# Attention scores as one fp32 product, and the feed-forward weight splits moved between stages

## The reference, cut to what matters

```python
h = tok(x)                                  # layer norm of shifted patches, times W
h = concat([cls_tok, h])                    # 16 x 37 x 192
n = layernorm(h)
q = n @ w_q.T + b_q; k = n @ w_k.T + b_k; v = n @ w_v.T + b_v
scores = einsum('bqhd,bkhd->bhqk', q, k) / sqrt(16) + mask
h = h + (softmax(scores) @ v) @ w_o.T + b_o
n = layernorm(h)
h = h + alpha * shared(n) + (1 - alpha) * routed(n)
```

## Time and profile before

| what | before |
|---|---|
| median of three runs | 172.95 us |
| the profiled execution's own time | 172.75 us |
| its span, first to last instruction | 170.9 us |
| mean granted TensorE clock | 0.970 of full |
| busy: PE, weight loads, DVE, ACT, POOL | 149.0, 115.8, 121.2, 90.8, 41.2 us |
| transfers | 16.89 MB, mean 99 GB/s |

### The profile page before, as it was taken

One profiled execution on the slowest core, in us unless ns is written; L12 is line 12 of the kernel. 1 busy time (PEld: TensorE's weight loads), 2 busy tenths in 40 slices (PEclk: granted clock), 3 DMA queues, 4 the chain that ended last, 5 costly groups with the idle time before them and its releaser, 6 DMA issues.

```text
span 170.9 us, 4275 instructions
## 1 busy us (share of the span) xinstructions
PE 149.0 (87%) x1714; PEld 115.8 (68%) x1714; DVE 121.2 (71%) x297; ACT 90.8 (53%) x198; POOL 41.2 (24%) x55
## 2 busy tenths in 40 slices
PE   0439999998899889669998689999899999999992
PEld 0218777943569778568954468788777778888781
DVE  6299969898999997933377399876795752533753
ACT  0598779544669255251328768666645444343340
POOL 0000010000000000000000044337947858578430
PEclk9999999999999999965699999999999999999999
DMA  5999946700000000029960000048100000000003
GB/s 165 390 362 364 333 86 196 312 3 0 0 0 4 4 4 4 4 45 391 333 249 0 4 0 0 8 172 335 62 4 0 0 0 4 4 0 4 0 0 106
DMA packets 7391, 16.89 MB, mean 99 GB/s; under 512 B 800, under 2 KB 3612, under 8 KB 7372
## 3 DMA queue, kind: packets, MB, share of 16 engines
q1 hardware_dynamic: 7012, 16.29, 27.3%
q10 hardware_dynamic: 360, 0.34, 0.7%
HBM read 16.15 MB, written 0.47 MB: 97 GB/s over the span
## 4 chain that ended last, share of the span: by engine, by line
PE 57%; DVE 24%; ACT 7%; issue 5%; ACTq 3%; POOL 2%; DVEq 0%; POOLq 0%
PE PS L582 20%; PE PS L610 11%; PE PS L324 3%; PE PS L415 3%; DVE xsq L1130 3%; DVE mx L1126 2%; DVE piece L968 2%; PE PS L477 2%; PE PS L345 2%; PE PS L347 2%; PE PS L348 2%; PE PS L427 2%; DVE hn L1053 2%; PE PS L311 2%; POOL vhl L865 1%
## 5 line engine op out<-in xcount | busy, mean ns | idle before, releaser
L874 POOL TENSOR_TENSOR kq<-vhl,kq 128x296 f16<-128x296 f32 x35 | 28.7, 819 | 93.8 <-ACT kq L826 93.8
L1271 DVE SCALAR_TENSOR_TENSOR vhl<-PS,vhl 128x296 f32<-128x296 f32 x36 | 16.7, 465 | 21.0 <-POOL vhl L865 12.1
L819 ACT ACTIVATE vhl<-PS 128x296 f32<-128x296 f32 x36 | 14.9, 416 | 26.2 <-PE PS L582 26.2
L826 ACT ACTIVATE kq<-vhl 128x296 f16<-128x296 f32 x36 | 16.0, 446 | 5.7 <-DVE vhl L1271 5.7
L865 POOL TENSOR_TENSOR vhl<-vhl,xs 128x296 f32<-128x296 f32 x14 | 12.6, 901 | 5.5 <-issue 4.8
L1260 DVE TENSOR_TENSOR vhl<-vhl,xs 64x296 f32<-64x296 f32 (+1 forms) x18 | 10.2, 566 | 2.8 <-ACT vhl L819 2.6
L582 PE MATMUL PS<-XAh,piece 128*128 128x296 f16 x48 | 10.0, 289 | 2.0 <-DVE vhl L1271 1.9
L582 PE MATMUL PS<-XAh,slab 128*128 128x296 f16 x48 | 10.0, 290 | 0.9 <-DVE vhl L1271 0.9
L345 PE MATMUL PS<-whl,xhl 128*128 128x193 f16 (+1 forms) x40 | 10.5, 262 | 0.0
L925 DVE SCALAR_TENSOR_TENSOR we<-slab,gbs,we 128x192 f32<-128x192 f32 x24 | 8.1, 409 | 3.3 <-ACT we L666 3.3
L347 PE MATMUL PS<-whl,xhl 128*128 128x193 f16 (+1 forms) x40 | 10.4, 261 | 0.0
(11 more groups left out here) (217 smaller groups left out, 409.0 us busy)
## 6 DMA issues: line engine op xcount, KB each, us to landing
slab<-in_w_inner_dram SPq DMA_DIRECT2D x3, 960.0 KB, 9.7
xs<-gate_rows_dram SPq DMA_DIRECT2D x8, 296.0 KB, 5.5
xs<-in_x_inner_dram SPq DMA_DIRECT2D x3, 592.0 KB, 10.7
stage<-in_f_a_dram SPq DMA_DIRECT2D x2, 768.0 KB, 4.7
stage<-in_f_b_dram SPq DMA_DIRECT2D x2, 768.0 KB, 6.3
stage<-in_f_d_dram SPq DMA_DIRECT2D x2, 576.0 KB, 8.0
xhl<-in_f_a_dram SPq DMA_DIRECT2D x1, 768.0 KB, 5.2
xhl<-in_f_b_dram SPq DMA_DIRECT2D x1, 768.0 KB, 6.9
```

The lines of the kernel that those rows point to most:

```text
L819: A(silu[:, i % 2, :], PS[:, 3 + 2 * (i % 2), 0:HALF], ACT.Silu, scale=1.0 / XW).then_inc(S["a_silu"], 1)
L826: A(ah[:, f % ABUF, half * HALF:(half + 1) * HALF], hf[:, i % 3, :], ACT.Copy).then_inc(S["a_ah"], 1)
L874: G.tensor_tensor(al[:, f % ABUF, cols], hf[:, i % 3, :], ah[:, f % ABUF, cols], ALU.subtract).then_inc(S["g_al"], 1)
L1271: V.scalar_tensor_tensor(out=hf[:, i % 3, :], in0=PS[:, 4 + 2 * (i % 2), 0:HALF], scalar=SH / XW, in1=src[:, i % 2, :], op0=ALU.mult, op1= ...
```

## The change

Keys and queries are written once, in fp32, by ACT (`K32`, `Q32`); `kq_low` is gone from DVE, and product `f` waits for ACT alone. A score is one fp32 product instead of two f16 products, with scale factors that suit. ACT runs steps 2 to 5 of `ffn_high` between and right behind the key and query copies, where it ran them behind all of these. DVE runs steps 0 to 2 of `ffn_low` in the part of the keys, queries and values and steps 3, 4 and 5 behind `differences(2)`, `differences(3)` and `normalise(2)`; before, steps 0 and 1 stood ahead of `differences(0)`, steps 2 to 4 ahead of `differences(3)` and step 5 behind `differences(3)` and `normalise(1)`. The `own_values` steps 4 to 7 stand behind `differences(0)` and `differences(1)`, two each. On PE `wo(0)` is issued before `av(6)`. The loop of the rounds on ACT is written in another way, but its instructions keep their order.

```diff
@@ -53,10 +53,11 @@
 PIECES = 3
 PT_ = FT // PIECES
 
-SX, SW, SPIX, SPW, SK, SQ, SP_, SV, SCTX, SH = 64.0, 64.0, 16.0, 256.0, 16.0, 4.0, 256.0, 16.0, 16.0, 16.0
+SX, SW, SPIX, SPW, SK, SH, QKS = 64.0, 64.0, 16.0, 256.0, 16.0, 16.0, 32.0
 XW = SX * SW
 
 GATE_STEP = 6
+ABUF = 3
 CONSTS = 128 + 2 * CHUNKS + 1 + D + GROUPS + EXPERTS
 FRONT = 3 * P
 
...
@@ -147,10 +148,9 @@
         WC = sb("WC", [CROWS, AW], F16)
 
         KFC = 2 * LANES * 4 * BLOCK
-        kh = xsq[:, KFC:KFC + GROUPS * N // 2].bitcast(F16).rearrange("p (g n) -> p g n", g=GROUPS)
-        kq = sb("kq", [P, 3 * GROUPS * N // 2 + 192])
-        kqv = kq[:, 0:3 * GROUPS * N // 2].bitcast(F16).rearrange("p (k g n) -> p k g n", k=3, g=GROUPS)
-        KK, Q1, Q2 = kqv[:, 0], kqv[:, 1], kqv[:, 2]
+        kq = sb("kq", [P, ABUF * NPAD])
+        K32 = xsq[:, KFC:KFC + GROUPS * N].rearrange("p (g n) -> p g n", g=GROUPS)
+        Q32 = kq[:, 0:GROUPS * N].rearrange("p (g n) -> p g n", g=GROUPS)
         vhl = sb("vhl", [P, IMAGES * LANES * VW])
         vv = vhl[0:BLOCK, :].rearrange("p (b r c) -> p b r c", b=IMAGES, r=LANES)
         SCOLS = 2 * BLOCK
...
@@ -407,7 +406,7 @@
                 c0 = (QC if q else KC) + g * P
                 if f >= 4:
                     q4, g4, half4 = kq_product(f - 4)
-                    pe.wait_ge(S["v_q2" if q4 else "v_kk"], GROUPS * half4 + g4 + 1)
+                    pe.wait_ge(S["a_q" if q4 else "a_k"], GROUPS * half4 + g4 + 1)
                 cols = slice(half * HALF, (half + 1) * HALF)
                 for i, (w, x) in enumerate(zip(wparts(c0, c0 + P), xparts(cols))):
                     if f in (0, 6):
...
@@ -440,13 +439,12 @@
                         b = 2 * (2 * u + pair) + bi
                         tok = slice(b * POSITIONS, (b + 1) * POSITIONS)
                         for g in range(GROUPS):
-                            for Q in (Q1, Q2):
-                                for r in range(LANES):
-                                    rows = slice(32 * r, 32 * r + 32)
-                                    col = pair * BLOCK + g * POSITIONS
-                                    last = mm(PS[64 * bi:64 * bi + POSITIONS, 3 + r, col:col + POSITIONS],
-                                              Q[rows, g, tok], KK[rows, g, tok], start=False, stop=(Q is Q2),
-                                              skip_group_check=True)
+                            for r in range(LANES):
+                                rows = slice(32 * r, 32 * r + 32)
+                                col = pair * BLOCK + g * POSITIONS
+                                last = mm(PS[64 * bi:64 * bi + POSITIONS, 3 + r, col:col + POSITIONS],
+                                          Q32[rows, g, tok], K32[rows, g, tok], start=False, stop=True,
+                                          skip_group_check=True)
                 last.then_inc(S["p_s"], 1)
 
             def pt(p):
...
@@ -506,8 +504,8 @@
                 values(i)
             pe.wait_ge(S["v_mk"], 1)
             pe.wait_ge(S["v_jr"], 2)
-            pe.wait_ge(S["v_kk"], 6)
-            pe.wait_ge(S["v_q2"], 6)
+            pe.wait_ge(S["a_k"], 6)
+            pe.wait_ge(S["a_q"], 6)
             scores(0)
             for i in range(4, 7):
                 values(i)
...
@@ -529,11 +527,11 @@
                 if u >= 2:
                     ct(2 * u - 4)
                     ct(2 * u - 3)
+            wo(0)
             av(6)
             av(7)
             ct(4)
             ct(5)
-            wo(0)
             wo(1)
             ct(6)
             ct(7)
...
@@ -750,9 +748,9 @@
                 cols = slice(half * HALF, (half + 1) * HALF)
                 act.wait_ge(S["p_q" if q else "p_k"], GROUPS * half + g + 1)
                 if q:
-                    A(Q1[:, g, cols], PS[:, 3 + f % 4, 0:HALF], ACT.Copy, scale=SQ / XW).then_inc(S["a_q1"], 1)
+                    A(Q32[:, g, cols], PS[:, 3 + f % 4, 0:HALF], ACT.Copy, scale=QKS / XW).then_inc(S["a_q"], 1)
                 else:
-                    A(kh[:, g, cols], PS[:, 3 + f % 4, 0:HALF], ACT.Copy, scale=kscale).then_inc(S["a_kh"], 1)
+                    A(K32[:, g, cols], PS[:, 3 + f % 4, 0:HALF], ACT.Copy, scale=1.0 / XW).then_inc(S["a_k"], 1)
 
             root(0)
             ffn_high(0, 0)
...
@@ -768,19 +766,21 @@
             high_parts(0, (1, 2, 0), 1)
             for f in range(3, 12):
                 kq_high(f)
+                if f in (5, 8):
+                    ffn_high(0, 2 + (f - 5) // 3)
+            ffn_high(0, 4)
+            ffn_high(0, 5)
 
             def exps(u):
                 act.wait_ge(S["v_sub"], u + 1)
                 if u >= 2:
                     act.wait_ge(S["p_pt"], 2 * u - 2)
-                A(prob[:, u % 2], sdif[:, u % 2], ACT.Exp, scale=1.0 / (SK * SQ * 4)).then_inc(S["a_exp"], 1)
+                A(prob[:, u % 2], sdif[:, u % 2], ACT.Exp, scale=1.0 / (8 * QKS)).then_inc(S["a_exp"], 1)
 
 
             A(vv[:, :, :, GROUPS * HD:VW].rearrange("p b r o -> p (b r) o"),
               bones[0:BLOCK, :].unsqueeze(1).to_broadcast([BLOCK, IMAGES * LANES, GROUPS]),
               ACT.Copy).then_inc(S["a_vh"], 1)
-            for q in range(2, 6):
-                ffn_high(0, q)
             exps(0)
 
             def ctx_high(i):
...
@@ -792,14 +792,15 @@
                 last.then_inc(S["a_chi"], 2)
 
             for u in range(4):
+                if u == 3:
+                    ctx_high(0)
                 for p in (2 * u, 2 * u + 1):
                     act.wait_ge(S["p_pt"], p + 1)
                     A(PT[:, p].rearrange("p r q -> p (r q)"), PS[0:BLOCK, (7, 0)[p % 2], 0:LANES * QROWS],
                       ACT.Copy).then_inc(S["a_pth"], 1)
                 if u < 3:
                     exps(u + 1)
-                if u >= 2:
-                    ctx_high(u - 2)
+            ctx_high(1)
             ctx_high(2)
             ctx_high(3)
             root(3)
...
@@ -1079,19 +1080,6 @@
             normed(0, range(3))
             variances(2)
 
-            def kq_low(f):
-
-                q, g, half = kq_product(f)
-                cols = slice(half * HALF, (half + 1) * HALF)
-                if q:
-                    dve.wait_ge(S["a_q1"], GROUPS * half + g + 1)
-                    V.scalar_tensor_tensor(out=Q2[:, g, cols], in0=PS[:, 3 + f % 4, 0:HALF], scalar=SQ / XW,
-                                           in1=Q1[:, g, cols], op0=ALU.mult, op1=ALU.subtract).then_inc(S["v_q2"], 1)
-                else:
-                    dve.wait_ge(S["a_kh"], GROUPS * half + g + 1)
-                    V.scalar_tensor_tensor(out=KK[:, g, cols], in0=PS[:, 3 + f % 4, 0:HALF], scalar=SK / XW,
-                                           in1=kh[:, g, cols], op0=ALU.mult, op1=ALU.add).then_inc(S["v_kk"], 1)
-
             def thrice(i, half):
 
                 R, X = ((RAh, XAh), (RAl, XAl), (RB, XB), (RC_, XC))[i]
...
@@ -1105,19 +1093,18 @@
             rsqrt(2)
             low_parts(0, (1, 2, 0), 0)
             normed(0, (3, 4))
-            attention_low(0, VC, AW)
-            kq_low(0)
-            attention_low(1, VC, AW)
-            attention_low(2, VC, AW)
-            kq_low(1)
-            kq_low(2)
+            for k in range(3):
+                attention_low(k, VC, AW)
+            ffn_low(0, 0)
+            thrice(0, 0)
+            thrice(1, 0)
             low_parts(0, (1, 2, 0), 1)
-            for f in range(3, 12):
-                kq_low(f)
-                if 3 <= f < 7:
-                    thrice(f - 3, 0)
-                if 7 <= f < 11:
-                    thrice(f - 7, 1)
+            thrice(2, 0)
+            thrice(3, 0)
+            for k in range(4):
+                thrice(k, 1)
+            ffn_low(0, 1)
+            ffn_low(0, 2)
 
             def differences(u):
 
...
@@ -1154,20 +1141,20 @@
 
             for i in range(4):
                 own_values(i)
-            ffn_low(0, 0)
-            ffn_low(0, 1)
             differences(0)
-            for i in range(4, 7):
-                own_values(i)
-            for u in range(4):
-                if u < 3:
-                    differences(u + 1)
-                if u == 0:
-                    own_values(7)
-                if u >= 1:
-                    normalise(u - 1)
-                for q in ((), (2, 3, 4), (5,), ())[u]:
-                    ffn_low(0, q)
+            own_values(4)
+            own_values(5)
+            differences(1)
+            own_values(6)
+            own_values(7)
+            differences(2)
+            normalise(0)
+            ffn_low(0, 3)
+            differences(3)
+            normalise(1)
+            ffn_low(0, 4)
+            normalise(2)
+            ffn_low(0, 5)
             def add_attention(t):
                 dve.wait_ge(S["p_wo"], (2, 2, 4, 4, 5)[t])
                 return V.scalar_tensor_tensor(
```

(5 more changed lines are left out.)

## The result

The changed kernel takes **166.84 us** in the median of four executions (168.43, 167.3, 165.86, 166.39), the kernel before, on the same chip between them, 173.51 (174.1, 172.95, 172.73, 174.07). The ratio is 0.96, with a 95% interval from 0.952 to 0.968: faster. The forecast was 166.6 us, in a range from 164.9 to 171.2.

A forecast was written before the change was run, and what follows sets the result against it. DVE splits hold the softmax chain by 1.9 us, and the clock halves behind PE's resulting gap. Softmax chain 1.8 plus clock 4.5 gives 6.3 us off 172.75, 166.45; plus 0.2 for the median, 166.6 us, range 164.9 to 171.2.

The forecast's parts named there:

- case (d): Whole kernel: the clock stays up and the path is the one worked out, forecast 166.6 us; chance 0.68.
- The clock falls behind the gap and stays up without it: PE behind round 3: idle stretch shrinks from 2.64 to 0.8 us, clock stays at 2.4 GHz, 4.5 us saved.
- Softmax chain: Attention rounds: with splits moved off DVE's way, maxima of round 3 start at 68.9 instead of 70.73, 1.8 us earlier.
- Up to the maxima of round 0: Round 0: earlier values and no split ahead, so maxima start at 56.45 instead of 57.52.
- The round was to grow: Ring of scores, maxima and differences: fp32 scores add 0.35 us a round, 3.78 to 4.13 us.
- My sum of columns: Score records on PE: fp32 takes 3 x 37 columns, 11.6 ns apart, 0.35 us more a round.
- Keys and queries: Key and query products on PE: no low parts to wait for, net gain 0.4 us, between 0 and 0.8.
- The wait at product 6: Key products: PE waits 0.25 to 0.3 us for DVE's low parts of the second half of the tokens.
- wo(0) and the last two splits at nothing: Behind round 3: wo(0) ahead of av(6) at most 0.3 us either way; last two splits cost nothing.
- Behind the residual all is unchanged: From the residual add (86.02) on: nothing changes, all moves as a whole.
- What would have shown it wrong: Signs: clock row still dips, a round takes over 4.5 us, or PE waits for ACT in the key products.
- Case (a): Rival, behind round 3: the clock falls all the same after the 0.8 us gap, leaving 1.8 us gain, 171.1; chance 0.15.

The follow-up runs named there:

- e2: The kernel before, with ten unread matmuls on PE ahead of the last transposes of round 3, no work moved: 169.14 us.
- e12: The changed kernel itself, run again without any edit: 166.5 us against 172.91 for the kernel before.
- e10: The kernel before (f16 scores) with splits moved behind the differences of round 3 and fills of three, one and three unread matmuls: 166.96 us.
- e7: The changed kernel with three unread matmuls ahead of the first key product and one ahead of its fourth matmul: 166.86 us.
- e3: The changed kernel with four splits (2 to 5) in one lump on DVE ahead of the differences of round 3: 171.62 us.
- e9: The changed kernel with only fp32 scores and key and query copies; splits, own_values and wo(0) in their old places: 172.3 us against 172.6 for before.
- e1: The kernel before with only feed-forward splits 2 to 4 moved behind the differences of round 3 on DVE, f16 scores kept: 166.98 us.
- e11: The kernel before, nothing moved, with three and one unread matmuls in the first gap and ten in the long gap of round 3: 169.21 us.
- e5: The changed kernel with each fp32 score product issued twice, 192 records a round instead of 96: 181.98 us.
- e6: The changed kernel with wo(0) put back behind ct(5) on PE: 166.4 us.

## Why the prediction was right

The median came out 0.2 us from the forecast, by case (d). Step by step:

**The clock falls behind the gap and stays up without it: shown.** Filling it alone (2), moving the splits alone (1), putting the gap back (3) and filling it again (4) all went as this step says in the medians, and fp32 alone (8) gave 0.3 us. The clock's price was put at 4.5 us, and `e2` measures 4.6.

**Softmax chain: right in kind, too small.** 1.8 us were forecast, 2.45 measured, from the earlier trace rows on:

- Up to the maxima of round 0 the gain was to be 1.07 us; it is 17.55 - 16.33 = 1.22 (16.33 in `e12`, maxima at 56.69).
- The round was to grow from 3.78 to 4.13 us; it is 3.87 in `e12` (the masks of rounds 2 and 3, 62.96 and 66.83) and 3.78 in `e10`. **This is the term that was mis-sized.** 96 records take 1.07 us and the last one 0.20, so they are 9.2 ns apart, against 7.9 in the earlier trace rows and the 11.6 that I built. The burst grew by 0.14 us and not by 0.35. My sum of columns, fitted on column tiles and on fp32 products two abreast, does not carry over to fp32 in row tiles.
- Maxima to maxima, rounds 0 to 3 took 13.21 us in before, with a lump in them, and take 11.98 now; the forecast had 12.45.

The Trainium skill (TensorEngine Tiling, Instruction Overhead), whose 60 cycles of overhead would have made it 0.14 us a round, came nearer than my sum; the 0.14 measured agree with it, though one shape alone is no test of the rule. It would have made the forecast 0.8 us lower, below the measured median.

**Keys and queries:** 0.4 us forecast, 0.39 measured: the mask of round 0 starts at 55.11 in `e12`, 14.75 from the first `hn`, and at 55.11 - 39.97 = 15.14 in before. The wait at product 6 was put at 0.25 to 0.3 us, and 0.27 were measured. TensorE did not wait for ACT's copies of keys and queries: products behind one another follow at 0.63 us in `e7`.

**wo(0) and the last two splits at nothing:** right, 39.09 against 39.16.

**Behind the residual all is unchanged:** wrong by 0.37 us, the one step that failed outright. In before the residual add is 84.88 us from the end of the span, in `e12` 85.28. The timeline of the second norm says where. Before:

```profile
88.54 0.21 ACT L727 ACTIVATE small<-small 128x5 f32<-128x5 f32 x1 [2.23 <-DVE small L1046]
...
88.85 0.19 DVE L994 RECIPROCAL small<-small 128x5 f32<-128x5 f32 x1 [0.34 <-ACT small L727]
```

The changed kernel:

```profile
83.82 0.21 ACT L725 ACTIVATE small<-small 128x5 f32<-128x5 f32 x1 [2.23 <-DVE small L1047]
84.50 0.19 DVE L995 RECIPROCAL small<-small 128x5 f32<-128x5 f32 x1 [0.71 <-ACT small L725]
```

DVE takes up the square root of ACT 0.10 us after it ends in before, and 0.47 us after in the changed kernel, with the same instructions around. All later work moves by these 0.37 us. It is so in each kernel with fp32 scores (0.70 to 0.72 of idle time in `e3` to `e9` and `e12`) and in none with f16 scores (0.34 in `e1`, `e2`, `e10` and `e11`). What delays DVE there was not tried; it belongs to the program and not to the execution.

**The sum.** Forecast 1.8 + 4.5 = 6.3. Measured on clean executions 2.45 + 4.60 = 7.05, less 0.16 that the chain gives back up to the residual (6.89), less 0.40 up to the end: 6.5. That the sum came so near is in part luck: an fp32 price too high by 0.2 us a round stood against a loss that I had not seen. Between before and `e12` the spans differ by 6.1, since the first `hn` is 0.4 us later in `e12`.

**What would have shown it wrong.** One of these signs came up: the clock row of the changed kernel does dip, but at 44 to 48 us, behind waits of 0.67 and 0.24 us at the first key product, in a stretch that the change leaves as it is. Case (a), given 0.15, asked for a fall behind the shortened gap of 0.9 to 1.0 us. It is in neither of the two profiles of the changed kernel (gaps of 0.89 and 0.98 us, both at 1.00 behind it). By the Trainium skill (TensorE: Matmul & The Clock Gate, Part 4), for which transposes do not count as work, what counts as idle in `e12` runs from the end of `av` at 70.4 to the next `av` at 72.86, about 2.4 us, against 4.9 in before (from 70.80 to 75.69); the clock held all the same. No run here separates this rule from the plain one.

**What the prediction did not see.** It treated the clock as a function of the schedule. It is a matter of odds. Of 33 executions of before, three ran at clocks of 0.986 to 1.00 and took 167.4 to 167.8 us; the others took 170.8 to 174.5, at 0.95 to 0.98 in all whose clock is on record. Of ten executions of the changed kernel, none took over 168.43. The change does not forbid the fall. It takes away the stretch behind which it nearly always came. What it gives beside the clock is 1.9 us: that much shorter is `e12` than `e2`, which is before with the gap filled, from the first `hn` to the end of the span (124.44 against 126.34).

**Open:** what stops TensorE inside a burst of small matmuls; which of several light stretches brings the clock down in a given execution; and the 0.37 us at the second norm.

## What to carry to other kernels

Where an engine off the path does a lump of work between two links of the path, look at what its delay opens on TensorE: here 2.6 us of splits held the path by 1.9 us and then cost 4.6 more in clock. Moving them by one tuple was worth nearly as much as the whole change, of which the rewritten scores alone gave 0.3 us. To tell whether a gap or the work in it matters, fill the gap with unread matmuls and change nothing else, and compare times counted from a point ahead of the change. A fill belongs in a stretch where TensorE waits anyway, and it should be short: where the clock had already fallen (`e11`), it delayed what it was to protect.

## What the runs showed of the hardware that was not expected

- An fp32 product of 32 x 37 against 32 x 37 in row tiles, four lanes, shows as two records 9.2 ns apart; the f16 one as one record, 7.9 ns apart. So an fp32 score costs about what two f16 passes do, and replaces them with no price worth counting (0.14 us in 96 records).
- TensorE can stop for 0.8 to 2.4 us inside a burst of small matmuls, with no releaser in the profile; in `e1` and `e5` nothing else was busy then, in `e11` DVE was. With 96 records in a burst it came in 2 of the 52 bursts profiled (0.97 us in `e1`, 1.00 in `e11`, both f16), with 192 in three of four (4.8 us in all in `e5`).
- A fall of the clock to 0.5 followed idle times of 3.17, 2.64 and 2.52 us, and also stretches with single stops of 1.0 us or of 0.67 and 0.24 us; idle times of 0.9 to 1.0 us elsewhere were passed at 1.00, and before and `e12` passed the same two waits at 1.00. Its price here was 1.4, 3.1 and 4.6 us.
- A fall can also be free. In `e2`, `e6` and `e9` the clock fell to about 0.5 for 3 to 4 us between 88 and 98 us, and the way from the residual add to the end of the span stayed at 84.89, 85.29 and 85.30 us, against 84.88 in before and 85.28 in `e12` without such a fall. A mean clock of 0.986 does not by itself say that time was lost.
